# A four-engine LoRA and prompt-pool kernel: later expansion weights, six early rows, and half-rows of values on GpSimd

## The reference

```python
x = x + (einsum('bsr,bdr->bsd', einsum('bsd,brd->bsr', x, A[lang]), Bm[lang]) + emb[lang][:, None, :])
attn_in = tanh(einsum('bsd,da->bsa', x, W1) + b1)          # A = 64
scores  = einsum('bsa,a->bs', attn_in, v)
mask    = {0: l <= j, 1: l >= j, 2: l != j}[kind]          # by row of the batch
p       = softmax(where(mask, scores[:, None, :], -1e30), axis=-1)
x = x + einsum('bjl,bld->bjd', p, x) / cnt[..., None]      # cnt: allowed l for each j
```

## Time and profile before

| what | value |
|---|---|
| median of 3 runs | 118.76 us (117.76 to 119.64) |
| profiled execution, own time | 118.1 us |
| its span | 116.3 us |
| PE, PE weight loads, DVE, ACT, POOL busy | 88%, 70%, 85%, 70%, 25% |
| mean granted TensorE clock | 0.973 |
| chain of waits by engine | DVE 42%, PE 32%, issue 11%, DMA 6%, ACT 5% |

### The profile page before, as it was taken

The page is one execution under the profiler, slowest core; times in us unless marked ns, Lnnn a source line. Parts: engine busy times, 40 slices in busy tenths (PEclk is TensorE's granted clock), DMA queues, the critical chain, the costliest instruction groups (busy, mean ns, idle before and its releaser), DMA issues.

```text
span 116.3 us, 2490 instructions
## 1 busy us (share of the span) xinstructions
PE 102.6 (88%) x606; PEld 81.6 (70%) x606; DVE 99.3 (85%) x244; ACT 81.5 (70%) x168; POOL 28.8 (25%) x84
## 2 busy tenths in 40 slices
PE   7939999999999999993999989999899989989930
PEld 2718788996989778881587666777687767767820
DVE  5724999999778899999839999968999999999980
ACT  1966755687699999984172877878878889885300
POOL 6736852235766682100030210000000000000000
PEclk9999999999999999999589999999999999999995
DMA  3999999999999999920002406413445253345463
GB/s 89 256 312 379 385 377 383 377 376 379 377 375 377 369 386 374 322 71 0 6 0 93 180 21 252 177 51 144 183 180 182 88 206 144 130 168 186 180 229 135
DMA packets 16104, 25.87 MB, mean 223 GB/s; under 512 B 1256, under 2 KB 10024, under 8 KB 16090
## 3 DMA queue, kind: packets, MB, share of 16 engines
q1 hardware_dynamic: 15912, 25.44, 61.6%
q10 hardware_dynamic: 178, 0.27, 0.8%
HBM read 17.25 MB, written 8.39 MB: 220 GB/s over the span
## 4 chain that ended last, share of the span: by engine, by line
DVE 42%; PE 32%; issue 11%; DMA 6%; ACT 5%; SPq 1%; DVEq 0%
DVE o L819 18%; PE psum L418 13%; DVE yl L773 10%; PE psum L493 8%; DMA xT<-in_x_t 6%; DVE x L722 5%; PE psum L427 4%; DVE tT L711 3%; PE psum L436 3%; ACT yh L616 2%; PE psum L468 2%; PE psum L472 2%; DVE rz L847 2%; ACT tT L582 2%; ACT tanh L589 1%
## 5 line engine op out<-in xcount | busy, mean ns | idle before, releaser
L493 PE MATMUL psum<-yh,q 128*128 128x258 f32 x128 | 34.9, 304 | 3.8 <-DVE o L819 3.3
L418 PE MATMUL psum<-xT,wsel 128*128 128x256 f32 x128 | 30.6, 382 | 1.9 <-DMA xT<-in_x_t 1.9
L493 PE MATMUL psum<-yl,q 128*128 128x258 f32 x128 | 32.1, 282 | 0.0
L493 PEld LDWEIGHTS psum<-yh,q 128*128 128x128 f32 x128 | 24.3, 190 | 8.7 <-issue 8.3
L624 ACT ACTIVATE q<-psum 128x512 fp32r<-128x512 f32 x32 | 19.1, 597 | 14.7 <-PE psum L472 14.6
L773 DVE SCALAR_TENSOR_TENSOR yl<-x,g_col,yh 128x258 fp32r<-128x258 f32 x64 | 29.3, 483 | 0.1
L616 ACT ACTIVATE yh<-x,g_col 128x258 fp32r<-128x258 f32 x64 | 28.9, 501 | 0.2
L418 PEld LDWEIGHTS psum<-xT,wsel 128*128 128x128 f32 x128 | 24.0, 190 | 5.6 <-DMA xT<-in_x_t 2.4
L819 DVE SCALAR_TENSOR_TENSOR o<-psum,rz,x 128x256 f32<-128x256 f32 x64 | 27.1, 481 | 0.5 <-DVE rz L830 0.3
L493 PEld LDWEIGHTS psum<-yl,q 128*128 128x128 f32 x128 | 24.4, 191 | 0.0
L351 POOL COPY wsel<-wall 128x256 f32 x32 | 13.0, 416 | 15.6 <-PE psum L418 12.6
(11 more groups left out here) (96 smaller groups left out, 72.6 us busy)
## 6 DMA issues: line engine op xcount, KB each, us to landing
xT<-in_x_t SPq DMA_DIRECT2D x16, 512.0 KB, 8.1
x<-in_x_n SPq DMA_DIRECT2D x16, 512.0 KB, 9.5
out<-o SPq DMA_DIRECT2D x31, 256.0 KB, 2.0
out<-o SPq DMA_DIRECT2D x2, 128.0 KB, 2.1
o<-in_b_nat ACTq DMA_DIRECT2D x1, 200.0 KB
w_in<-in_w_pack SPq DMA_DIRECT2D x1, 196.5 KB, 2.5
n_arg<-n_part SPq DMA_DIRECT2D x8, 4.0 KB
m_arg<-m_part SPq DMA_DIRECT2D x8, 4.0 KB
```

The source lines that it names most:

```text
L418: last = nc.tensor.matmul(proj_ps[b // 2 % 2][:, b % 2 * S:(b % 2 + 1) * S], wsel[:, b % V, c, :], xT[:, b % RING, c, :], start=(c == 0), ...
L493: last = nc.tensor.matmul(pool_ps[SLOTS[b]][:, j, 0:DZ], q[:, b % V, s, j * P:(j + 1) * P], part_y[:, b % VY, s, :], start=(s + k == 0), s ...
```

## The change

- ACT issues the load of the expansion weights behind its wait for `w_in`, not ahead of it.
- POOL reads two languages, not four, before its first select, and its memsets for `x1`, `forbidden` and `rounds` stand behind select(3). ACT waits for these at step 5, not before step 0.
- `ON_POOL` becomes (7, 9, 11).
- Of the early rows six are left (NE = 6): `high_y(6)` and `high_y(7)` go to b = 0 and 1 of ACT's second part, their `low_y` to the end of b = 2 and 3 on DVE.
- `fraction(0, 1)` stands behind `low_t(5)`.
- PE issues two matmuls of constants into bank 6 (filler) between the value loads and `expand(30)`.
- Of rows 15, 17, ... 31 the second half of `yl` is made by POOL, in two instructions (`half`): a tensor_scalar into `half_y`, which lies in the first buffer of `xT`, and a tensor_tensor. It starts at the rz of pair b for row b + 5, and PE waits for it.
- In `output_pair` both halves of `low_y(b+4)` stand between zc and rz.

```diff
     EARLY_STEP = 7
-    ON_POOL = (11, 13, 15, 17)
+    NE = 6
+    ON_POOL = (7, 9, 11)
     SLOTS = [b % 2 if b < R0 else (b - R0) % 3 for b in range(B)]
...
         b_in = o[0:K, 2:4, :, :].rearrange("p v c d -> p (v c d)")
+        half_y = xT[:, 0, :, :].rearrange("p c n -> p (c n)")[:, 0:DZ]
         wall = sb("wall", [P, L, ND, M])
...
         yl_ready = sem("yl_ready")
+        half_whole = sem("half_whole")
+        half_ready = sem("half_ready")
         pooled = sem("pooled")
...
             return b - FIRST[group(b)]
+
+        def pool_half(b):
+            return R0 + LEAD < b < B and (b - R0 - LEAD) % 2 == 1
+
+        def pool_halves(b):
+            return len([a for a in range(b) if pool_half(a)])
...
             nc.gpsimd.tensor_scalar(sign[:], low[:], -2.0, 1.0, ALU.mult, ALU.add).then_inc(signs_ready, 1)
-            nc.gpsimd.memset(x1[:, 0:B // 2, :, D:DZ], 1.0)
-            nc.gpsimd.memset(x1[:, B // 2:B, :, D:DZ], 1.0).then_inc(tails_ready, 1)
-            for t, value in ((0, 1.0), (1, 0.0), (2, 2.0)):
-                nc.gpsimd.memset(forbidden[:, t:t + 1], value)
-            nc.gpsimd.memset(rounds[:, 0:1], ROUND)
-            nc.gpsimd.memset(rounds[:, 1:2], -ROUND).then_inc(tails_ready, 1)
...
             pool.wait_ge(ids_loaded, 16)
-            first = [language(b) for b in range(V)]
+            first = [language(b) for b in range(2)]
             pool.wait_ge(wall_ready, 3)
             for b in range(B):
-                select(b, first[b] if b < V else language(b))
+                select(b, first[b] if b < 2 else language(b))
                 if b == 3:
+                    nc.gpsimd.memset(x1[:, 0:B // 2, :, D:DZ], 1.0)
+                    nc.gpsimd.memset(x1[:, B // 2:B, :, D:DZ], 1.0).then_inc(tails_ready, 1)
+                    for t, value in ((0, 1.0), (1, 0.0), (2, 2.0)):
+                        nc.gpsimd.memset(forbidden[:, t:t + 1], value)
+                    nc.gpsimd.memset(rounds[:, 0:1], ROUND)
+                    nc.gpsimd.memset(rounds[:, 1:2], -ROUND).then_inc(tails_ready, 1)
                     nc.gpsimd.affine_select(out=identb[:], in_=ones[:], compare_op=ALU.is_equal, fill=0.0, base=0,
...
+            def half(b, k):
+                n = pool_halves(b)
+                pool.wait_ge(r_ready, k)
+                if n == 0:
+                    pool.wait_ge(projected, B)
+                    pool.wait_ge(g_ready, 2)
+                else:
+                    pool.wait_ge(half_ready, n)
+                nc.gpsimd.tensor_scalar(half_y, x1[:, b, 1, :], g_col[:, 1, 1, local(b):local(b) + 1], None, ALU.mult
+                                        ).then_inc(half_whole, 1)
+                pool.wait_ge(half_whole, n + 1)
+                pool.wait_ge(yh_ready, b + 1)
+                pool.wait_ge(pooled, b - VY + 1)
+                nc.gpsimd.tensor_tensor(yl[:, b % VY, 1, :], half_y, yh[:, b % VY, 1, :].bitcast(fp32), ALU.subtract
+                                        ).then_inc(half_ready, 1)
+
+            for b in range(R0, B - 2, 2):
+                if pool_half(b + LEAD + 1):
+                    half(b + LEAD + 1, R0 + 1 + (b - R0) // 2)
+
         @block.tensor
...
-            def keep_warm(n):
+            def keep_warm(n, of=7):
                 for _ in range(n):
-                    nc.tensor.matmul(bank[7][:, :], nc.const_aps.tensor(1.0, (P, P), bf16),
+                    nc.tensor.matmul(bank[of][:, :], nc.const_aps.tensor(1.0, (P, P), bf16),
                                      nc.const_aps.tensor(1.0, (P, NS * S), bf16), start=True, stop=True)
...
                 pe.wait_ge(yl_ready, b + 1)
+                if pool_half(b):
+                    pe.wait_ge(half_ready, pool_halves(b) + 1)
                 if b == 0:
...
             kinds = [kind_of(0), kind_of(1)]
+            pe.wait_ge(g_ready, 1)
+            keep_warm(2, 6)
             expand(B - 2, langs[0])
...
             act.dma_start(biasL[L:L + 1, F0:F0 + A], b1).then_inc(b1_loaded, 16)
-            act.dma_start(b_in, b_nat).then_inc(b_loaded, 16)
             act.wait_ge(consts, 1)
...
             act.wait_ge(w_loaded, 16)
+            act.dma_start(b_in, b_nat).then_inc(b_loaded, 16)
             for k in range(REP):
...
             act.wait_ge(tT_ones, 1)
-            act.wait_ge(tails_ready, 3)
...
                 if p == 5:
+                    act.wait_ge(tails_ready, 3)
                     whole(0)
...
                 squash(2 * p + 1)
-                if EARLY_STEP <= p < EARLY_STEP + FIRST[1]:
+                if EARLY_STEP <= p < EARLY_STEP + NE:
                     high_y(p - EARLY_STEP)
...
                     grow(0)
-                if p == NP - 1:
-                    for k in range(p - EARLY_STEP + 1, FIRST[1]):
-                        high_y(k)
             powers(0)
...
                     powers(b + 2)
+                if b < FIRST[1] - NE:
+                    high_y(NE + b)
                 if b == 1:
...
             def low_y(b, s):
-                if b >= B:
+                if b >= B or pool_half(b) and s == 1:
                     return
...
                                                      ALU.mult, ALU.subtract)
-                if s == NS - 1:
+                if s == NS - 1 or pool_half(b):
                     ins.then_inc(yl_ready, 1)
...
                     fraction(0, 0)
+                low_t(p)
+                if p == 5:
                     fraction(0, 1)
-                low_t(p)
                 if p >= 1:
...
                     maximum(0, p - 6)
-                if EARLY_STEP < p <= EARLY_STEP + FIRST[1]:
+                if EARLY_STEP < p <= EARLY_STEP + NE:
                     for s in range(NS):
...
             add_lora(NP - 1)
-            for k in range(NP - EARLY_STEP - 1, FIRST[1]):
-                for s in range(NS):
-                    low_y(k, s)
...
                 ins.then_inc(z_ready, 1)
-                low_y(b + LEAD, 0)
+                for s in range(NS):
+                    low_y(b + LEAD, s)
                 dve.wait_ge(z_ready, k)
                 nc.vector.reciprocal(rz[:], zc[:]).then_inc(r_ready, 1)
-                low_y(b + LEAD, 1)
                 divide(b, k)
...
                     maximum(1, 3)
+                if b in (2, 3):
+                    for s in range(NS):
+                        low_y(NE + b - 2, s)
             for b in range(R0, B - 2, 2):
...

```

## The result

| | before | after |
|---|---|---|
| median of four runs each, us | 118.50 (117.76 to 119.64) | 123.22 (122.99 to 124.14) |
| profiled execution, us | 118.1 | 123.01 |
| its span, us | 116.3 | 121.2 |

The changed kernel is slower: ratio 1.0434, 95% interval 1.0346 to 1.0522. The forecast was 120.2, its range ended at 121.5. The lines that answer to those of before follow in the order of the kernel; in the changed kernel `project` is L448, `expand` L457, the filler L471, `pool_rows` L525, `low_t` L744, `add_lora` L755, `low_y` L806, `o` L850, `zc` L857, L870 and L874.

A forecast was written before the change was run, and what follows sets the result against it. Stages decide: value loads hold PE at the first's end, DVE fills the second and binds the third by 0.13. Profiled 118.1 + 0.34 (up to expand(30)) + 1.6 (rows) + 0.2 (pairs) = 120.2; 8-in-10 range 117.0 to 121.5.

The forecast's parts named there:

- the weights: Start, before expand(0): later issue of the expansion weights makes expand(0) late by 0.6, bounds -0.2 to 0.9.
- rival E: Start: the expansion weights land in time, term 0 instead of 0.6, total 119.6; chance 0.12.
- rival B: End of first stage: the clock stays up instead of falling, -1.4, total 118.8; chance 0.22.
- The fractions and ON_POOL: First stage, p = 6: PE's 0.48 wait goes, as low_t(5) no longer stands behind both fractions: -0.44.
- this contention at the `yl`: First stage, DVE: POOL's copies can now meet a pair of yl and slow it: +0.15.
- The pacing by ACT and DVE: First stage, steps after p = 6: counted forward, low_t(14) comes at 50.56 instead of 50.99: -0.43.
- The four value loads: End of first stage: they stand ahead of expand(30) in PE's sequencer and hold it 3.19 after expand(28), unchanged.
- The filler: End of first stage: two matmuls ahead of expand(30) don't fill the idle stretch and cost +0.46, bounds 0 and 0.9.
- Rows 6 and 7: Moved from first to second stage: no gain at expand(30), four yl at 0.40 on a full DVE, +1.6.
- Rival D: Second stage, rows 3 to 5: the clock falls a second time, about 1.0 more, total 121.2; chance 0.12.
- The pairs: Third stage: the loop through PE binds at 3.31, DVE's own sum 3.04; +0.02 in each of nine periods, +0.2.
- Rival C: Third stage: pairs follow DVE's own sum, period 3.04 instead of 3.31, -2.5, total 117.7; chance 0.16.

The follow-up runs named there:

- the run with eight: The changed kernel with the expansion weights loaded early, and all eight early rows in the first stage again (NE = 8): 116.84, ratio 0.99.
- the two above: Kernels without POOL's halves: one with early weights, eight early rows, second yl behind the four o, value loads spread (117.78); the changed kernel with early weights (120.12).

## Why the prediction was right in its direction and wrong in its size

**The step that failed: the weights.** The prediction took 0.6 and bounded the term by "shifted by the whole 1.24 ... 0.9 late". Both came from moving the arrival by as much as the issue. It was 3.54 at expand(0). What was overlooked is that two loads of 512 KB, which had landed behind the weights, would land ahead of them once they are issued 1.18 later; the prediction let the xT in front come earlier, as its lower end, but didn't count them as work in front. The second part of the same error is the clock: the prediction had no idle time and no fall there, but PE then idled 2.93, and step 2 ran at half speed: 1.70 more, which did not come in the run with SP held, where the clock stayed up. With 5.24 for 0.6 the miss of this term, 4.6, is larger than that of the whole forecast.

The Trainium skill (DMA: Bandwidth & Descriptors, "Queues, rings and completion order") says that each DMA engine takes the queues in turn by packets, and by that the term would have been nearer 0. No run here agrees with that consequence: on ACT's queue, with nothing of SP's on it, the weights of the changed kernel moved hardly a packet until 7 us, four after their issue. With less issued in front they began within one (the run with SP held). The prediction named the rule beside its 0.6, and its rival E, with a term of 0, was further off still.

**The clock at the end of the first stage: rival B's event.** The forecast had it fall, at a chance of 0.22 for staying up; it stayed up, in the changed kernel and in most of the experiments. That gave back 1.16 in the profiled execution (B: 1.4) and hides part of the miss above. The runs of before beside the experiments had both: 25 with a mean clock of 0.979 or less at a median of 118.0, 17 at 0.998 or more at 117.5, so by the run times the fall is worth nearer 0.6; why two traces give twice that is open. What decides it isn't settled. The idle stretch was 2.02 in before (fell), 2.04 after (up), 2.03 with old order and eight rows (fell), 2.02 without the filler (up) and 2.02 with the second `yl` behind the four o (up). In four others it was 1.79 to 1.81, all up.

**The fractions and ON_POOL: -0.44 predicted, -0.20 measured,** and nothing in the kernel with early weights (project(14) at 27.92 for 27.99, project(12) at 24.64 for 24.70), where PE still loses the same 0.48 before the weight load of p = 6 (26.60). The order of the fractions did what it should, but ON_POOL's new rows put a half of add_lora on POOL beside the small caps of group 0 on DVE. POOL's timeline of the kernel with early weights:

```profile
23.57 1.19 POOL L382 TENSOR_TENSOR x<-carry,x 128x512 f32<-128x512 f32 x1
```

DVE's:

```profile
23.79 0.99 DVE L762 CAST kindr<-kindr_i 24x2 f32<-24x2 int32 x1
```

A cast of 24x2, 0.15 in before, took 0.99 and ended at 24.78, when POOL's ended (24.76). In the changed kernel it is the next instruction, of 24x6, with 1.12 (28.96 to 30.08, POOL 28.88 to 30.06). The prediction had looked for this contention at the `yl`, for 0.15. In the first stage there is none there (0.87 or 0.88 for each pair of `yl`); it was on the smallest instructions of the stage. The Trainium skill (SBUF — State Buffer, "SBUF: two separate sides") has a DVE instruction of two SBUF inputs wait for a whole GpSimd one that reads SBUF and began first; the trace agrees for the 24x6, which has two. The cast has one; whether it falls under the rule's other case, a mode that uses both ports, no row shows. The pacing by ACT and DVE behind it was -0.43 predicted, -0.38 measured.

**The four value loads** held expand(30) as said: 3.24 and 3.19 whatever the values and the filler did, 1.68 without them. low_t(15) was free of blame with six early rows. The filler, +0.46 in the sum, was 0.05. The prediction said that it doesn't fill the idle stretch; in part it does. With early weights its two matmuls start at 54.32, 0.26 ahead of expand(30) and behind 1.81 of idle; without it PE idles 2.02.

**Rows 6 and 7**: +1.6 predicted, 1.74 in the profile, 1.7 by the run with eight. Right, with the mechanism: four `yl` on a full DVE. The 0.14 above is the first pair, which takes 1.02 at 69.54 where the second takes 0.87; a POOL cast runs beside it (69.68 to 70.28). Rival D, a second fall of the clock in rows 3 to 5, did not come; PE idled 1.31 there (before 71.89) at full clock.

**The pairs**: +0.2 predicted, +0.24 measured, by the mechanism given: period 3.31 (3.35), DVE waiting 0.25 (0.20) for PE, pieces 1.07, 1.02, 1.22 (1.09, 1.02, 1.24). Rival C was wrong here, and its number, 3.04, is what the pairs take once the `yl` is out of the loop. The length of POOL's half was off: its tensor_scalar takes 0.94 and not 0.3 to 0.6, the whole 1.67 and not 1.2 to 1.5. It cost nothing, as it ended before it was needed.

**The end** was -0.6 and not in the sum at all. Terms together: weights and clock +4.64, fractions, pacing and contention +0.14, filler -0.41, clock at the end of the stage -1.16, rows and pairs +0.18, end -0.6: +2.8, which is the 123.0 of the profiled execution less 120.2.

## What to carry to other kernels

When a DMA is moved to a later issue, don't move its arrival by the same amount. Read from the trace when the loads of the other queues around it land, ask which of them will now land first, and divide their bytes by the rate that the page shows for that stretch; here two loads of 512 KB were 3.6 us. That holds for the changed kernel; the same move in before cost 4.3 at hB, and with SP held the weights came 1.2 later than the shift of their issue, and nothing here gives a rule for either. Then ask whether the idle time that this makes on PE lowers the granted clock behind it. Work given to an idle engine pays only if it comes off what binds: here a loop from zc to o to PE's next row bound by 0.1 to 0.3, and the same half on POOL was worth 1.6 or 4.2 by whether a `yl` stood inside that loop or behind it. Early weights, eight early rows, POOL's halves and the second `yl` behind the four o make 113.6, 3.8% faster than before (ratio 0.9624, 0.9541 to 0.9708).

## What the runs showed of the hardware that was not expected

- A load of 200 KB on ACT's queue, issued 1.18 later, arrived 3.6 later: two loads of 512 KB on SP's queue that had landed behind it now landed ahead of it. With the second of these held back until the same moment its first packets moved within one us, but the last needed about six (10.45 for hB).
- DVE instructions of 24x2 and 24x6 elements were held up to 1.0 by a POOL tensor_tensor and ended with it (24.78 and 24.76; 30.08 and 30.06).
- The granted clock fell or stayed up behind nearly the same idle stretch (2.02 to 2.04), even among runs of one kernel. Behind 2.93 idle (after) and 4.51 (the late weights in before) it was 0.50 in the next step; with SP held PE idled 2.21 at that place and the page's row shows no dip.
- The clock's rows say 1.00 from the start of the span, but in the changed kernel the matmuls of 256 columns stand 0.43 apart until about 10 us and 0.22 from there on; in before the full pace is there from 4.3.
- POOL's tensor_scalar of 128x258 with a scalar per partition takes 0.94, longer than its tensor_tensor of the same size, 0.64.
- With POOL's halves the end is shorter, though nothing in it was changed: from zc(28) to the end of the span it is 7.4 in the four kernels without halves (before, before with late weights, and the two above) and 6.7 to 6.8 in the ten with them. In DVE's timeline of before the last o stands 0.27 idle behind its rz,

```profile
112.68 0.88 DVE L819 SCALAR_TENSOR_TENSOR o<-psum,rz,x 128x256 f32<-128x256 f32 x2 [0.27 <-DVE rz L830]
```

and in the changed kernel it doesn't; the last stores land in 2.1 and 1.8. The waits for the buffers of the outputs would fit, since pairs that wait for PE leave them more time, but the kernel with a period of 3.04 has the short end too. The cause stays open.
